# Products that nobody reads, issued by TensorE in the first period of the last layers of a decoder kernel

## The reference

```python
xn = _layernorm(x, ln1_g, ln1_b)
q, k, v = xn @ Wq, xn @ Wk, xn @ Wv           # normalised, rotated
gj = -softplus(xn @ gate_w + gate_b)          # "forms": gate, clock, p
clock = softplus(xn @ clock_w + clock_b)
p = xn @ p_w + p_b
...
scores = einsum('bqhd,bkhd->bhqk', q, k) / sqrt(Dh)
attn = softmax(where(mask, scores, -inf))
out = einsum('bhqk,bkhd->bqhd', attn, v)
```

## Time and profile before

| what | us |
|---|---|
| time, median of 3 runs | 1292.72 (1290.24 to 1295.18) |
| the profiled execution's own time | 1288.51 |
| its span | 1286.8 |
| TensorE busy (share of the span) | 1123.6 (87%) |
| VectorE busy | 743.7 (58%) |
| ScalarE busy | 544.2 (42%) |
| GpSimd busy | 459.7 (36%) |
| mean granted TensorE clock | 0.949 |

### The profile page before, as it was taken

The page is one execution under the profiler, slowest core; times in us unless marked ns, Lnnn a source line. Parts: engine busy times, 40 slices in busy tenths (PEclk is TensorE's granted clock), DMA queues, the critical chain, the costliest instruction groups (busy, mean ns, idle before and its releaser), DMA issues. The chain is left out here.

```text
span 1286.8 us, 20425 instructions
## 1 busy us (share of the span) xinstructions
PE 1123.6 (87%) x6750; PEld 796.0 (62%) x6750; DVE 743.7 (58%) x2260; ACT 544.2 (42%) x1407; POOL 459.7 (36%) x539
## 2 busy tenths in 40 slices
PE   7889988998899797799999937788898899789996
PEld 3466455644654576799999924454655575466775
DVE  1473367247534855455555637758748576856366
ACT  1371246125521741333333317466465457543541
POOL 0251025004400784566666541424221522222122
PEclk9999999999999998899999959689998999899999
DMA  5000010020001013741111141101000100000000
GB/s 194 17 1 1 28 46 2 1 56 17 1 1 56 2 55 124 266 145 48 45 50 51 42 141 39 33 1 29 5 8 1 34 9 17 1 1 25 1 1 33
DMA packets 40228, 52.38 MB, mean 41 GB/s; under 512 B 10780, under 2 KB 33372, under 8 KB 40124
## 3 DMA queue, kind: packets, MB, share of 16 engines
q1 hardware_dynamic: 31100, 36.66, 8.8%
q0 software_dynamic: 3408, 9.31, 2.6%
q10 hardware_dynamic: 5616, 5.11, 1.2%
HBM read 41.76 MB, written 9.31 MB: 40 GB/s over the span
## 5 line engine op out<-in xcount | busy, mean ns | idle before, releaser
L1631 PE MATMUL bank<-words 128*128 128x256 f32 (+3 forms) x872 | 276.1, 469 | 26.7 <-DVE words L2639 9.1
L1631 PEld LDWEIGHTS bank<-words 128*128 128x128 f32 (+1 forms) x872 | 166.7, 198 | 112.7 <-issue 58.0
L419 PE MATMUL bank<-words 128*128 128x512 f32 x384 | 171.6, 598 | 8.2 <-DMA words<-in_wq 8.2
L371 POOL TENSOR_TENSOR words<-words 128x256 f32<-128x256 f32 (+1 forms) x128 | 103.6, 831 | 176.3 <-DVE words L972 176.3
L1182 PEld LDWEIGHTS bank<-words 128*128 128x128 f32 x1248 | 147.4, 194 | 3.5 <-ACT words L1216 1.6
L1182 PE MATMUL bank<-words 128*128 128x128 f32 x1248 | 147.9, 277 | 0.9 <-ACT words L1216 0.9
L754 ACT ACTIVATE words<-words 128x128 f32<-128x128 f32 (+1 forms) x256 | 113.3, 444 | 52.8 <-DVE words L967 52.8
L419 PEld LDWEIGHTS bank<-words 128*128 128x128 f32 x384 | 72.1, 192 | 89.5 <-issue 88.9
L706 ACT ACTIVATE words<-bank 128x512 f32<-128x512 f32 x48 | 28.7, 598 | 191.0 <-PE bank L419 191.0
L1231 ACT ACTIVATE words<-words 128x1024 f32 x39 | 41.1, 1057 | 144.4 <-PE bank L1182 127.9
L808 DVE COPY words<-bank 128x512 f32<-128x512 f32 x48 | 33.2, 691 | 104.6 <-PE bank L419 104.3
(11 more groups left out here) (346 smaller groups left out, 2013.6 us busy)
## 6 DMA issues: line engine op xcount, KB each, us to landing
words<-in_w SPq DMA_DIRECT2D x8, 1024.0 KB, 9.7
y_slots<-words ACTq DMA_DIRECT2D x39, 128.0 KB, 1.7
words<-in_w SPq DMA_DIRECT2D x8, 512.0 KB, 10.1
words<-in_xt SPq DMA_DIRECT2D x4, 512.0 KB, 3.8
words<-in_x SPq DMA_DIRECT2D x4, 512.0 KB, 4.1
x_rows<-words SPq DMA_DIRECT2D x16, 128.0 KB, 1.8
words<-in_wm SPq DMA_DIRECT2D x2, 1024.0 KB, 6.9
out_x<-words SPq DMA_DIRECT2D x16, 128.0 KB, 1.8
```

The costliest lines, as they stand in the source:

```text
L371: last = pool.tensor_tensor(part, part, inv[:, j % SLOTS0, :, t:t + 1].to_broadcast([P, 2, P * (t + 1)]), ALU.mult)
L419: last = pe.matmul(bank[c % 2][:, :], w, r, start=k == 0, stop=k == KD - 1)
L1631: last = pe.matmul(out, w, r, start=i == 0, stop=i == len(pairs) - 1)
```

## The change

A helper `keep_busy(count, n, width)` is added to TensorE's program. Each call issues `count` products of the identity with the first `width` columns of a weight tile that has long been in memory, into bank `n`. Nobody reads that bank before it is overwritten, and no semaphore is touched. It is called at several places of period 0; nothing else changes on any engine.

```diff
             pe.wait_ge(early, NE1 * 16)
+            def keep_busy(count, n=5, width=512):
+                for _ in range(count):
+                    pe.matmul(bank[n][:, 0:width], ident[:, :], wqk[:, 0, 0:width], start=True, stop=True)
...
+            keep_busy(11, 7)
             turn(0, n4, 0, lambda t: xn[:, t, :], bank[2])
+            keep_busy(1, 7)
             pe.wait_ge(n4.copied, 1)
             first_form(0, 0)
             first_form(0, 1)
+            keep_busy(4, 7)
             turn(0, n4, 1, lambda t: xn[:, t, :], bank[3])
...
             for b in range(GB):
                 pe.wait_ge(turning, HALF * b + HALF)
                 first_turns(b)
+                if b == 0:
+                    keep_busy(2)
                 pe.wait_ge(qkt, HALF * b + HALF)
+                if b == 1:
+                    keep_busy(1)
                 for j in range(PAIRS1 // GB + 3):
                     if j < PAIRS1 // GB:
                         scores(0, (PAIRS1 // GB * b + j,))
                     if j >= 3 and j % 2:
                         weighted(0, QUADS1 // GB * b + (j - 3) // 2)
+                        keep_busy(1, width=256)
+                    else:
+                        keep_busy(1)
+            keep_busy(3)
             turn_front(1)
```

## The result

| | changed | before |
|---|---|---|
| time, median of 4 runs | 1311.86 us (1307.45 to 1314.66) | 1291.81 us (1290.24 to 1295.18) |
| ratio, with its 95% interval | 1.0152 (1.0120 to 1.0183) | |
| the profiled execution's own time | 1307.45 us | 1288.51 us |
| its span | 1305.7 us | 1286.8 us |
| TensorE busy | 1162.5 us (89%) | 1123.6 us (87%) |

The change makes the kernel 1.5% slower. The forecast was 1287.2 us, 0.4% faster. The granted clock did rise, and the time went up with it.

The account below looks back on a forecast made before the run. It took period 0 to be bound by TensorE's short pieces standing in the chain at half clock. Gains of 0.7 + 1.85 + 1.4 + 1.5 = 5.45 us, from the 1292.7 us median, gave 1287.2 us; overall range 1283 to 1291.5.

Parts of the forecast that it names:

- term B: First sequence's scores: shorter waits for scores and quicker transposes at full clock gain 1.85 us, between 0 and 2.5.
- term C: Second sequence's scores: up to the last minimum's end 1.4 us are gained, between 0.5 and 2.2.
- rival 3: Second sequence's scores: filling gets in the way at half clock, 8 us added, 1296.6 us; chance 0.08 together with rival 4.
- rival 4: Added products do nothing for the clock, as operands never change or nobody reads them; gains vanish; counted with rival 3, 0.08.
- The eleven products: Ahead of the first turn: they take 11.1 or 12.5 us and hide in 13.1 us of room.
- Term A: First forms of period 0: quicker second turn and form at full clock gain 0.7 us, between 0 and 1.4.
- Term D: End of period 0: quicker turns, head transposes, forms and their products at full clock gain 1.5 us, between 0 and 1.7.
- at full clock it just fits: Ahead of the turn ending period 0: added products of 3.9 us leave TensorE free at 841.2, the turn coming at 841.36.
- rival 2: Clock lost in two gaps, before the second turn and at the late transposes: 3.2 us stay, 1289.5 us; chance 0.14.
- The forward shift: From 848 us on TensorE is busy without a pause, so the time gained in period 0 goes to the end.

Follow-up runs that it names:

- e16_change: The change again, unaltered, against the kernel before on the fourth chip: 1294.05 us, ratio 1.0080.
- e15_before: The kernel before, unaltered, profiled on the fourth chip: 1284.32 us.
- e13_pairs: The change with its products moved so none stands between a pair's two units, against the kernel before on the fourth chip: 1285.29 us, ratio 0.9997.
- e4_pairs: The change with as many products but none between a pair's two units, against the kernel before on the first chip: 1293.83 us, ratio 0.9998.
- e2_scores: Only the added products of the two attentions kept, against the kernel before on the first chip: 1311.77 us, ratio 1.0137.
- e12_thin: Only the products among the scores kept, cut to 32 columns, against the kernel before on the third chip: 1295.61 us, ratio 1.0084.
- e9_change: The change again, unaltered, against the kernel before on the third chip: 1289.19 us, ratio 1.0045.
- e11_burst: The change with six products ahead of the second qkt wait instead of one behind it, against the kernel before on the third chip: 1290.24 us, ratio 1.0035.
- e6_weights: The change with real weights instead of the identity, against the kernel before on the second chip: 1286.23, 1292.52, 1302.36 and 1303.70 us, ratio 1.0097.
- e10_weights: The change with real weights instead of the identity, against the kernel before on the third chip: 1294.24 us, ratio 1.0070.
- e7_first: The change with the loop's products in the first sequence alone, against the kernel before on the second chip: 1288.68 us, ratio 1.0008.
- e1_front: Only the 11, 1 and 4 products around the first forms kept, against the kernel before on the first chip: 1293.08 us, ratio 1.0000.
- e3_tail: Only the three products ahead of `turn_front(1)` kept, against the kernel before on the first chip: 1292.47 us, ratio 0.9993.
- e14_waits: Change with unparted pairs, four products ahead of the second qkt wait, one ahead of the next group's turn, against the kernel before: 1285.51 us, ratio 1.0002.

## Why the prediction was wrong

**The price of a unit of scores (terms B and C, rival 3).** The failed step is "TensorE per two units 0.95 for scores, 0.86 for `weighted`, 0.86 and 0.43 for the filling: 3.1 us". The 0.95 us come from a row of sixteen records, two units together. By the code even units use rows 0 to 63 of the array and odd ones rows 64 to 127, and eight records alone take 0.92 us. Two units overlap when neither a product nor a wait stands between them; the change put a product between every two. The rows that had shown filling to work, period 1's, have their products between pairs and never inside one (`scores(a, (2 * q, 2 * q + 1))` in the code); in the trace of before:

```profile
904.76 0.94 PE L1686 MATMUL bank<-words 32*128 32x256 f32 x16
905.63 0.86 PE L1697 MATMUL bank<-words 128*32 128x256 f32 x16
906.42 2.00 PE L1751 MATMUL bank<-words 128*128 128x256 f32 x8
908.40 0.94 PE L1686 MATMUL bank<-words 32*128 32x256 f32 x16
```

Measured, the two units and what goes with them take 4.2 us at full clock, against 3.1. Of the 1.1 us more, 0.76 are the scores (twice 0.855 from start to start, less 0.95); the rest is nearly all in the products, 1.05 and 0.63 us from start to start behind tiles of 32 rows instead of 0.86 and 0.43. That makes TensorE the pace in both sequences, not "by about 0.5 us over two units".

At full clock this alone turns B and C over. On the fourth chip, from the first scores to the first sequence's last minimum it is 16.3 us in e16_change against 15.3 in e15_before, and from the second sequence's first minimum to its last one's end 14.8 against 12.5: 3.3 us lost, where 3.25 were to be won. e13_pairs, with the same work as e16_change on the same chip and no parting, shows no loss, and neither does e4_pairs beside e2_scores; that is what makes parting the cause. e12_thin shows that a product of 32 columns parts two units as one of 512 does.

**The clock (rival 3).** I had its condition, half clock through the second sequence, and gave it 8 in 100 with rival 4, with the argument that "TensorE would then be busy without a pause, and such stretches got the full clock in every row here". The rows behind that were of full products. It did not hold for this mix: 0.50 at 32.31 of 33.50 us busy here, and at 50.48 of 54.00 in e12_thin. With the units unparted the clock rose again 6.0 us after the restart in e4_pairs and 4.1 us in e13_pairs. A clock that was full the parted units did not lose: it is 1.00 through both attentions in e9_change, e11_burst and e16_change. (In e12_thin it fell 1.4 us after the restart that followed 2.26 us of idle time.) So the parted units did not only cost more in a given clock; once the clock had fallen they went with it staying down until the last `weighted`. That the order of the same work decides it is what the changed kernel and e4_pairs show between them; what in the order the chip reacts to stays open. In size this is the greater part: the faster executions of e9_change and e16_change are 3 to 4 us above the kernel before, and the rest of the result's 20 us comes only with the half clock.

Rival 3's price was also too small: 5.8 us per two units are 7.8 measured, for the same reason. It gave 8 us more than before for the second sequence; the profile has 14.3 more from the first minimum to the last.

**What makes the clock fall ahead of the second sequence.** In the result's profile TensorE idles 6.67 us there: VectorE gets the transposed rows 5.0 us late, though TensorE's transposes start at 816.92 and take 1.10 us. The clock fell at about 823.1, inside this idle time. All four profiles of the first chip have that wait too, with the loop's products or without; none of the twelve of the other three chips has it, for the kernel before and the changed one. On which chip the result itself was profiled is not on record. With it, in the result and on the first chip, the changed kernel and e2_scores have all their executions above 1307 us (four of each). Where it isn't, TensorE idles 2 us and the change's executions split, the middles of the two groups 14 to 16 us apart. That the slower ones are those that lose the clock there was not profiled; it is worked out: 33.5 us at half clock in 1290 are 0.013 of the mean clock, and 0.973 less 0.013 is 0.960, within the 0.956 to 0.962 of the slower executions. It does not explain four executions of 1292.52 to 1298.87 us (e6_weights, e10_weights and two of e16_change), whose clocks of 0.968 to 0.972 are nearly those of the short ones; what they lost stays open. e11_burst supports it: with the gap filled none of eleven was long. So does e13_pairs, in whose profile 1.98 us of idle at that place did lose the clock: it fell at about 820.9, 0.7 us after the restart, and was full again from 824.3. In e7_first, after the same 1.99 us, it held there. What delays the hand-over to VectorE by 5 us stays open. The kernel before was not profiled on a chip that has the wait, so its own profiles can't tell what it loses there; e1_front and e3_tail equal it on such a chip. For the same reason the 4.3 us of late hand-over in the table above can't be charged to the change.

**The eleven products** hid as forecast: the clock rose at about 748.0, 3.9 us after their start, and the first turn was still released by ScalarE, 15.71 us after the expert layer against 15.81:

```profile
744.10 11.38 PE L1822 MATMUL bank<-words 128*128 128x512 f32 x22 [2.87 <-PEq L1077]
756.94 0.84 PE L1640 MATMUL bank<-words 128*128 128x128 f32 x4 [1.47 <-ACT words L2257]
...
767.63 0.83 PE L1640 MATMUL bank<-words 128*128 128x128 f32 x4 [3.31 <-ACT words L2257]
```

**Term A** (0.7 us, between 0 and 1.4) was 0.2 us here: the clock fell at about 768.5, behind the idle 3.31 us, and the first scores came at +55.86 against +56.02. In e16_change the clock had fallen at 756.9 and was back at 760.3; it then held through the 2.46 us of idle at 767.80, and the scores came at +54.88. So both ends of the term were real, and it gave 0.2 or 1.1 us. Neither can be told in e1_front's time (1.0000, with an interval of some 1.6 us on each side).

**Term B** (1.85) was -1.0 us up to the last minimum (from 56.02 to 71.25 before, from 55.86 to 72.13 after), **term C** (1.4) was -20.5 with the way between the sequences. Of that, 14.3 are the parted units at half clock and 6.3 lie between: the hand-over that is 4.3 us later than in the profile of before (5.0 against 0.7 us), and the one product behind the wait for `qkt`, 2.07 us at half clock where I had counted 0.86.

**Term D** (1.5 us) came out at 0.6: the forms behind the turn are at full clock, 3.70 us instead of 4.70, and the stretch from the turn to their end is 2.3 us shorter; but "at full clock it just fits" failed for the products ahead of the turn. The last `weighted` ended 3.6 us behind the last minimum (855.37 to 858.93), where the prediction had it end 1.7 us behind (835.56 to 837.3): the clock was half until 857 and 2.14 us of products stood ahead of it. Behind it stand ten records, of 256 and 512 columns:

```profile
858.07 0.86 PE L1697 MATMUL bank<-words 128*32 128x256 f32 x16
858.86 4.13 PE L1822 MATMUL bank<-words 128*128 128x256 f32 x10
862.83 1.04 PE L1640 MATMUL bank<-words 128*128 128x128 f32 x8
863.70 1.04 PE L1648 MATMUL bank<-words 128*128 128x128 f32 x8
865.45 3.70 PE L1631 MATMUL bank<-words 128*128 128x512 f32 x8 [0.72 <-ACT words L2218]
```

The turn has no idle time ahead of it: TensorE's own queue releases it, 1.7 us late (at full clock, in e16_change against e15_before, 0.4 us), which the prediction named as a sign of being wrong. These rows also answer rival 2. Transposes alone fill 862.83 to 864.7, and the clock is 1.00 there and in the forms behind. The rule of the Trainium skill (TensorE: Matmul & The Clock Gate, section on PE-mode transpose), that the full clock does not engage for transposes, did not have the outcome I had worked out from it: 1.9 us of them and the 0.72 us of idle time behind did not lose the clock. Whether transposes alone could raise it no run here shows.

**Why there is no gain even without the loss.** e13_pairs has the clock at 0.971 in its profile and nothing parted, and still runs as the kernel before. Counted in us from the first turn, its profile and that of e15_before are nearly level at every station:

| us from the first turn | e15_before | e13_pairs | e14_waits |
|---|---|---|---|
| first scores | 40.2 | 40.3 | 40.3 |
| end of the first sequence's last minimum | 55.5 | 54.9 | 54.9 |
| second sequence's first minimum | 64.2 | 64.6 | 63.9 |
| its last minimum's end | 76.7 | 76.7 | 76.0 |
| `turn_front(1)` | 82.5 | 83.2 | 81.8 |
| start of what follows the first forms | 89.6 | 89.6 | 88.9 |

Of term B 0.6 us came. e13_pairs lost it again at the second sequence's start, behind a product that began as the clock fell (1.42 us), and its turn came 0.7 us later behind the same ten records, which the faster forms gave back. e14_waits, with its products ahead of the second wait and fewer ahead of the turn, keeps 0.7 us, which is 0.05% and below what can be told. VectorE's wait for scores, forecast to fall from 6.6 to about 4 us, is 9.1 us in e13_pairs against 7.3 in e15_before; the longest, 3.1 us, lies behind that same product. So B, C and D were sized too high even for an order that parts nothing.

**The forward shift** held: what is gained or lost in period 0 goes through unchanged (436.7 against 437.0 us behind the first forms).

## What to carry to other kernels

Before putting anything between two instructions, see in the count of a row and in its duration whether they run side by side: here two units on different rows of the array took 0.95 us together and 0.92 each when one product, of 32 or of 512 columns, stood between them. When an example elsewhere in the trace is the model for a change, check that the order is the same and not only the mix. Filling goes into waits that exist, ahead of a wait rather than behind it, and should end before the next turn could start. A higher mean clock is no gain by itself: here it rose from 0.949 to 0.964 while the time rose by 1.5%.

## What the runs showed of the hardware

- Once the clock had fallen, it stayed at 0.50 through parted units of 32-row scores with full products between them, TensorE 96% busy over 33.5 us (93% over 54 us with products of 32 columns). The same work with the two units adjacent was at full clock 6.0 us after its restart (e4_pairs). Parted units that began at full clock kept it (e9_change, e16_change).
- One kernel's executions on one chip fell mostly into two groups 14 to 16 us apart; the mean clock fits one gap of 2 us having lost the clock or not, and no execution of the long group was profiled. The median of such a kernel depends on how many fall into which: the change gave 1.0152, 1.0045 and 1.0080 in its three comparisons.
- A product whose moving operand never changes and whose stationary operand is the identity raised the clock as one of real weights did: it rose 3.5 us after the eleven had started in e9_change and 3.9 us in e10_weights.
- VectorE waited 3.7 to 5.2 us for the transposed rows in all four profiles of one chip, and 0.3 to 1.3 us in all twelve of three others; the profile names no releaser for the long wait.
